# Chunked scan of a two-layer network: carried part of y scaled on its way out of PSUM, decays of all chunks worked out ahead, state scaled by ScalarE

## The reference

```python
dA = jnp.minimum(jnp.exp(dt * A[None, None, :]), 0.99)
def step(h, inp):
    x_t, B_t, C_t, dA_t = inp
    dBx = jnp.einsum('bhp,bn->bhpn', x_t, B_t)
    h = jnp.clip(dA_t[:, :, None, None] * h + dBx, -10.0, 10.0)
    y_t = jnp.einsum('bn,bhpn->bhp', C_t, h)
    return (h, y_t)
```

## Time and profile before

| | us |
|---|---|
| median of 3 runs | 1801.12 |
| the profiled execution, its own time | 1799.88 |
| its span in the profile | 1797.9 |
| TensorE busy | 1697.8 (94% of the span) |
| VectorE busy | 1588.3 (88%) |
| ScalarE busy | 1475.2 (82%) |
| the scan's chunks, from the first sums to the last maxima | about 1562 to 1704 |

### The profile page before, as it was taken

One profiled execution on the slowest core, in us unless ns is written; L12 is line 12 of the kernel. 1 busy time (PEld: TensorE's weight loads), 2 busy tenths in 40 slices (PEclk: granted clock), 3 DMA queues, 4 the chain that ended last, 5 costly groups with the idle time before them and its releaser, 6 DMA issues.

```text
span 1797.9 us, 40083 instructions
## 1 busy us (share of the span) xinstructions
PE 1697.8 (94%) x15396; PEld 660.0 (37%) x15396; DVE 1588.3 (88%) x2294; ACT 1475.2 (82%) x2806; POOL 642.7 (36%) x932
## 2 busy tenths in 40 slices
PE   6899999999999999999999999999999889899894
PEld 4432222222222222278722222222222345466663
DVE  7999999999999999945499999999998477588679
ACT  6689999999999999943389999999999757777555
POOL 2432300222444444100035566555610133123347
PEclk9999999999999999999999999999999989899887
DMA  4522221111211222278512211122102243422121
GB/s 127 176 72 88 86 74 59 57 59 39 72 57 55 59 69 61 69 209 227 153 47 57 64 48 48 50 64 56 41 12 57 68 125 112 138 69 71 40 76 47
DMA packets 152765, 142.15 MB, mean 79 GB/s; under 512 B 40394, under 2 KB 131533, under 8 KB 152418
## 3 DMA queue, kind: packets, MB, share of 16 engines
q1 hardware_dynamic: 144226, 122.37, 23.7%
q0 software_dynamic: 8352, 17.29, 3.3%
HBM read 76.60 MB, written 60.03 MB: 76 GB/s over the span
## 4 chain that ended last, share of the span: by engine, by line
PE 80%; ACT 9%; DVE 7%; issue 2%; POOL 1%; DMA 1%; SPq 0%; DVEq 0%; ACTq 0%
PE PS L2051 29%; PE PS L2150 18%; PE PS L2035 11%; ACT probs L1361 6%; PE PS L2100 4%; DVE mxp L910 3%; PE PS L2085 2%; PE PS L2355 2%; PE PS L2337 2%; PE PS L2273 1%; PE PS L2194 1%; PE PS L2200 1%; PE PS L2358 1%; PE PS L2077 1%; PE PS L2434 1%
## 5 line engine op out<-in xcount | busy, mean ns | idle before, releaser
L910 DVE TENSOR_REDUCE mxp<-PS 128x1 f32<-128x1024 f32 x1024 | 1170.5, 1215 | 19.0 <-PE PS L2035 14.6
L1361 ACT ACTIVATE probs<-PS 128x512 f32<-128x512 f32 x2048 | 1096.0, 597 | 65.4 <-PE PS L2150 21.4
L2051 PE MATMUL PS<-probs,VH 128*32 128x256 f32 x8192 | 642.0, 391 | 2.3 <-ACT probs L1361 1.0
L2150 PE MATMUL PS<-stacks 51*128 51x512 bf16 x2048 | 441.4, 388 | 20.3 <-ACT probs L1361 15.7
L2035 PE MATMUL PS<-stacks 48*128 48x512 bf16 x2048 | 416.5, 380 | 2.7 <-DVE mxp L910 1.7
L2051 PEld LDWEIGHTS PS<-probs,VH 128*32 128x32 f32 x8192 | 172.7, 108 | 404.5 <-issue 224.2
L2150 PEld LDWEIGHTS PS<-stacks 51*128 51x128 bf16 x2048 | 115.9, 93 | 459.9 <-ACT probs L1361 385.4
L1727 POOL DMA_INDIRECT S<-oe_d,ROWI x128 | 129.8, 1014 | 133.8 <-PE PS L2051 127.6
L1697 POOL DMA_INDIRECT xe_d<-S,ROWI x128 | 125.2, 978 | 137.8 <-PE PS L2051 119.5
L1675 POOL CAST spl<-nmx 128x8 bf16<-128x8 f32 x64 | 12.6, 197 | 303.5 <-DVE nmx L866 225.3
L2035 PEld LDWEIGHTS PS<-stacks 48*128 48x128 bf16 x2048 | 105.4, 95 | 16.9 <-DVE mxp L910 7.4
(11 more groups left out here) (363 smaller groups left out, 1813.7 us busy)
## 6 DMA issues: line engine op xcount, KB each, us to landing
stacks<-qkl_d SPq DMA_DIRECT2D x128, 96.0 KB
xe_d<-zt SPq DMA_DIRECT2D x16, 640.0 KB
XNT<-xe_d SPq DMA_DIRECT2D x32, 320.0 KB, 3.8
oe_d<-XNT SPq DMA_DIRECT2D x32, 320.0 KB, 3.3
stacks<-qkl_d SPq DMA_DIRECT2D x128, 64.0 KB
o_d<-SG SPq DMA_DIRECT2D x256, 32.0 KB
ews<-in_ew_dram SPq DMA_DIRECT2D x33, 192.0 KB, 2.4
stacks<-qkl_d SPq DMA_DIRECT2D x128, 32.0 KB
```

What stands on the lines that cost most here:

```text
L910: v.tensor_reduce(mxp[:, n // 2, n % 2:n % 2 + 1], MXB[n % 2].rearrange("p a c -> p (a c)"), X_AX, ALU.max).then_inc(mx_done, 1)
L1361: act.activation(probs[:, at:at + 512], PS[:, bank_of(u, e), :], ACT.Exp, scale=float(1.0 / np.sqrt(np.float32(DK)))).then_inc(exp_done, 1)
L2051: mm = pe.matmul(OB[32 * jg:32 * jg + 32, c:c + 256], VH[w][:, kt, :], probs[:, at:at + 256], start=(kt < 2 and half == 0), stop=(kt >= TC ...
L2150: pe.matmul(PS[:, bank_of(u, e), :], KS[w][o:o + KROWS + 3, kt * P:(kt + 1) * P], QS[w][o:o + KROWS + 3, q0:q0 + 512], start=True, stop=Tr ...
```

## The change

- The decays of all 16 chunks are summed once, ahead of the loop (`all_sums_`, eight matmul instructions in bank 5), and ScalarE takes their exponentials once (`all_exps`, four operations): `EC` (per token, for y), `ET` (per chunk, for the state), `ER` (rows for the bound). `ER` is stored to DRAM and read back as rows in four pieces (`load_rows`, two DMAs each, in SyncE's queue between the chunks' loads).
- The per-chunk L2340, L1551, L1552, L1553, L1096, L1120 and L1123 go, and L2358 with its 8 products.
- The carried part of y is now C times the unscaled state: one product per sequence, 256 columns wide, into bank 2 and bank 7 (`CY`). ScalarE copies it to `YS` in eight operations (2 sequences, 4 heads, 128x64 each) with the decay of the token as a per-partition scale. VectorE adds the part inside the chunk to it from banks 3 and 4. The old copy L1564 goes.
- The state is scaled by ScalarE in four operations of 128x64.
- TensorE waits, ahead of the second L2330, until ScalarE has read `CY` (`cy_out`), since both use bank 2. ScalarE's order is: exponentials and squares of c + 1, carried part of c, state of c, turned `DM` of c + 1, bound of c.

The diff, cut to its core:

```diff
             def spread_decays(c):
                 after(v, la_ready, c)
-                link(v.tensor_copy(ldc[:, :, :].unsqueeze(2), ldt[:, :, c:c + 1, :]))
-                v.tensor_tensor(lb, TRI..., ldc..., ALU.mult).then_inc(lb_set, 1)
+                v.tensor_tensor(lb..., TRI..., ldt[:, :, c, :].unsqueeze(3).broadcast_to([P, B, NH1, P]), ALU.mult).then_inc(lb_set, 1)
...
-                v.wait_ge(el_done, c + 1)
-                v.tensor_tensor(CTD[w], E2[w], cc, ALU.mult).then_inc(ops_ready, 1)
             def chunk_state(c):
-                v.tensor_tensor(hst2[:, :, :], HS[:, :, :], E2[c % 2][:, :, P - 1:P]..., ALU.mult).then_inc(hst_set, 1)
                 v.wait_ge(hst_set, HALVES + c + 1)
-                v.wait_ge(y_out, c + 1)
+                v.wait_ge(yc_ready, c + 1)
                 v.tensor_tensor(HS[:, :, :], hst2[:, :, :], PS[:, 3, DI:2 * DI]..., ALU.add).then_inc(hs_done, 1)
+                v.wait_ge(cy_out, c + 1)
+                yc = YS.rearrange("p (b c) n -> p b c n", b=B)[:, :, c:c + 1, :]
+                v.tensor_tensor(yc, yc, PS[:, 3:5, 0:DI].unsqueeze(2), ALU.add).then_inc(y_out, 1)
...
+            def all_exps():
+                act.wait_ge(all_sums, ALL_BASE + 1)
+                act.activation(EC, PS[:, 5, 0:NT * NH1], ACT.Exp)
+                act.activation(ET, PS[:, 5, 2 * P:2 * P + TCH * NH1], ACT.Exp)
+                act.activation(ER[:, 1:P], PS[:, 5, P:2 * P - 1], ACT.Exp)
+                act.activation(ER[:, 0:1], PS[:, 5, 2 * P - 1:2 * P], ACT.Exp).then_inc(rows_out, 1)
...
+            def state_scaled(c):
+                after(act, hs_done, c)
+                for h in range(NH1):
+                    ins = act.activation(hst2[:, h, :], HS[:, h, :], ACT.Copy, scale=ET[:, c * NH1 + h:c * NH1 + h + 1])
+                ins.then_inc(hst_set, 1)
+            def carried(c):
+                act.wait_ge(cy_ready, c + 1)
+                for b in range(B):
+                    for h in range(NH1):
+                        col = (b * TCH + c) * NH1 + h
+                        ins = act.activation(YS[:, b * TCH + c, h * HP:(h + 1) * HP], CY[b][:, h * HP:(h + 1) * HP], ACT.Copy, scale=EC[:, col:col + 1])
+                ins.then_inc(cy_out, 1)
...
             chunk_exps(0)
+            all_exps()
             router_exp()
+            chunk_turned(0)
             for c in range(TCH):
                 if c + 1 < TCH:
                     chunk_exps(c + 1)
+                carried(c)
+                state_scaled(c)
+                if c + 1 < TCH:
+                    chunk_turned(c + 1)
                 chunk_out(c)
...
             def chunk_products(c):
                 pe.wait_ge(ops_ready, c + 1)
                 if c + 1 < TCH:
                     turned(c + 1, 0)
+                carried(c)
                 after(pe, y_out, c)
-                after(pe, hs_done, c)
...
-                for h in range(NH1):
-                    for b in range(B):
-                        mm = pe.matmul(PS[:, 3 + b, h * HP:(h + 1) * HP], CTD[w][rows_of(b), h, :], HS[rows_of(b), h, :], start=False, stop=(h == NH1 - 1))
                 mm.then_inc(yc_ready, 1)
+                if c == ROUTER_CHUNK or c + 1 < TCH:
+                    pe.wait_ge(cy_out, c + 1)
                 if c == ROUTER_CHUNK:
                     router_rows()
                 if c + 1 < TCH:
                     turned(c + 1, 1)
...
+            hold(rows_out, ROWS_OUT + 1)
+            sp.dma_start(er_d.rearrange("b (n t) -> (b n) t", t=P), ER).then_inc(rows_st, 16)
             for w in range(2):
                 hold(zx_st[w], 32 * NT // 2)
             hold(bct_st, 32 * NB)
-            for c in range(2, TCH):
+            hold(rows_st, ROWS_ST + 16)
+            load_rows(0)
+            load_chunk(2)
+            load_chunk(3)
+            load_rows(1)
+            for c in range(4, TCH):
+                if c in (7, 11):
+                    load_rows(c // 4 + 1)
                 load_chunk(c)
```

More of the change, by code:

```diff
@@ L254, in build @@
         by_head = lambda t: t.rearrange("p (h t) -> p h t", h=NH1)
-        E2 = [by_head(probs[:, 0:512]), by_head(ym_flat[:, 2560:3072])]
-        CTD = [by_head(probs[:, 512:1024]), by_head(ym_flat[:, 3072:3584])]
-        E2b = [by_head(wa[2 + i].rearrange("p t c -> p (t c)")[:, 0:256].bitcast(BF16)) for i in range(2)]
+        EC, ET, ER = probs[:, 0:NT * NH1], probs[:, 128:128 + TCH * NH1], probs[:, 192:256].bitcast(BF16)
+        ERB = [waq[:, 2 * i:2 * i + 2, :, :].rearrange("p i t c -> p (i t c)").bitcast(BF16) for i in range(2)]
+        E2b = [t.rearrange("p (c h t) -> p c h t", c=TCH // 4, h=NH1) for t in ERB]
         XS = [probs[:, 1024:1536], probs[:, 1536:2048], SG[0][:, :], SG[1][:, :]]
@@ L263, in build @@
         BD = [heads(t) for t in (probs[:, 3072:3584], ym_flat[:, 2048:2560])]
-        ldc = sb("ldc", [P, B, NH1])
+        CY = [PS[:, 2, 2 * P:2 * P + DI], PS[:, 7, 0:DI]]
         HS = sb("HS", [P, NH1, HP])
@@ L380, in build @@
         SH_BASE = 2 * NB
-        yl_ready, pr_ready, s2_done = (
-            sem(n) for n in ("yl_ready", "pr_ready", "s2_done"))
+        yl_ready, pr_ready, cy_out = (
+            sem(n) for n in ("yl_ready", "pr_ready", "cy_out"))
         a1_ready, a1_out, l1_ready, oh_ready = (
@@ L654, in load_chunk, with load_rows @@
                 sp.dma_start(XS[w].rearrange("p (b n) -> p b n", b=B), bview(xs_d)).then_inc(tile_ld[w], 16)
+            def load_rows(k):
+                hold(c_done, 4 * (k - 1) if k >= 2 else 0)
+                for b in range(B):
+                    sp.dma_start(ERB[k % 2][b * DS:b * DS + 1, :], er_d[b:b + 1, k * 4 * NH1 * P:(k + 1) * 4 * NH1 * P]).then_inc(er_ld[k % 2], 16)
             def store_b_c(j):
@@ L1557, in chunk_exps, with chunk_turned @@
                     act.activation(RB[w][:, b, :, HP:P], BS[c % 4][:, b, :].unsqueeze(1).broadcast_to([P, NH1, DS]), ACT.Square)
+            def chunk_turned(c):
+                w = c % 2
                 act.wait_ge(dm_done, c + 1)
@@ L2336, in chunk_sums, with all_sums_, carried @@
                 for b in range(B):
-                    pe.matmul(PS[:, b, :], BELOW, scaled[:, b, :], start=True, stop=True)
-                after(pe, el_done, c)
-                for b in range(B):
-                    mm = pe.matmul(PS[rows_of(b), 7, :], onesq[:, 0:DS], scaled[:, b, :], start=True, stop=True)
-                mm.then_inc(la_ready, 1)
+                    mm = pe.matmul(PS[:, b, :], BELOW, scaled[:, b, :], start=True, stop=True)
+                mm.then_inc(la_ready, 1)
+            def all_sums_():
+                pe.wait_ge(zx_out, 2 * NT)
+                decays = DT.rearrange("p t h -> p (t h)")
+                pe.matmul(PS[:, 5, 0:P], TRI, decays, start=True, stop=True)
+                pe.matmul(PS[:, 5, P:2 * P], decays, TRI, start=True, stop=True)
+                for b in range(B):
+                    mm = pe.matmul(PS[rows_of(b), 5, 2 * P:2 * P + TCH * NH1], onesq[:, 0:DS], decays[:, b * TCH * NH1:(b + 1) * TCH * NH1], start=True, stop=True)
+                mm.then_inc(all_sums, 1)
+            def carried(c):
+                after(pe, cy_out, c)
+                after(pe, hs_done, c)
+                for b in range(B):
+                    mm = pe.matmul(CY[b], BCT[c % 4][rows_of(b), P:2 * P], HS[rows_of(b), :, :].rearrange("p h n -> p (h n)"), start=True, stop=True)
+                mm.then_inc(cy_ready, 1)
             def chunk_products(c):
@@ L2366, in chunk_products @@
                 for b, h, n in pairs:
-                    pe.matmul(PS[:, 5 + b, h * P:(h + 1) * P], DMb[w][:, b * NH1 + h, :], RB[w][:, b, h, :], start=(h == 0), stop=False)
+                    mm = pe.matmul(PS[:, 5 + b, h * P:(h + 1) * P], DMb[w][:, b * NH1 + h, :], RB[w][:, b, h, :], start=(h == 0), stop=(c == 0 and h == NH1 - 1))
                 after(pe, vr_out, 2 * c)
-                for b, h, n in pairs:
+                if c:
+                    pe.wait_ge(er_ld[c // 4 % 2], ER_BASE + 32 * (c // 8 + 1))
+                for b, h, n in pairs if c else ():
                     r = slice(b * DS, b * DS + 1)
-                    mm = pe.matmul(PS[:, 5 + b, h * P:(h + 1) * P], E2b[w][r, h, :], VR[r, h, :], start=False, stop=(h == NH1 - 1))
+                    mm = pe.matmul(PS[:, 5 + b, h * P:(h + 1) * P], E2b[c // 4 % 2][r, c % 4, h, :], VR[r, h, :], start=False, stop=(h == NH1 - 1))
                 mm.then_inc(c_done, 1)
```

37 lines of the change are left out of this document (18 added, 19 removed).

## The result

The changed kernel takes 1787.78 us (median of 4 runs, 1784.49 to 1789.78) against 1800.42 for the kernel before in the same comparison: ratio 0.9925, 95% interval 0.9911 to 0.9940. Forecast were 1786.4 us, and -14.7; measured -12.6. The profiled execution ran 1787.86, its span is 1785.9.

A forecast was written before the change was run, and what follows sets the result against it. TensorE bound the scan at 8.09 us per chunk; afterwards a TensorE-ScalarE round trip of 7.2 us would. Start -0.7, trips -10.7 and end -3.3 gave -14.7: median 1786.4 us, 8-in-10 range 1779 to 1796.

The forecast's parts named there:

- The trip: Mid-scan loop from ScalarE's exponential through the carried copies, TensorE's wait and next sums, back to ScalarE: 7.2 us per chunk.
- The price taken as half of two pointers: ScalarE's short operations, 64 columns with one scale pointer: 0.225 us from start to start, bounds 0.18 and 0.32.
- The engines' own sums: Busy time per chunk after the change: TensorE 6.54 us (7.0 at the other bound), VectorE 6.5, ScalarE 6.9.
- TensorE last at 6.6: Rival: cheaper ScalarE operations leave TensorE's own sum, 6.54 to 6.8 us, as the trip; 1777 to 1781 us, chance 0.14.
- no overlap on ScalarE: Rival: ScalarE's pointer operations take 0.32 us each, its trip 8.0; 1797 to 1800 us, close to no change, chance 0.08.
- The clock: Rival: short waits per chunk drop TensorE to half clock, +3.7 us a chunk, at worst 1855 us, chance 0.06.
- 14 trips: Scan, chunk 1 to 15: 100.8 us, plus 0.4 for the router and 2.0 for chunk 2's data; 103.2 against 113.9.
- My evidence against it: Against the clock's fall: a stretch with TensorE busy 6.24 of 8.00 us had clock 1.00; here 6.5 of 7.2.
- Chunk 2's wait: Chunk 2's loads land 1.1 to 1.9 us later, behind `ER`'s store and rows; TensorE loses 1.5 to 2.7, taken +2.0.
- The start: Chunk 1: L2340 goes (-1.0 us), the eight products of all decays cost +0.3; -0.7 in all.
- The last chunk: From chunk 15's exponential to the last maxima: 12.4 us, 14.6 with half clock, taken 13.5; -3.3.
- The rest: The stage after the scan: unchanged, only beginning earlier.

The follow-up runs named there:

- e_state_dve: The changed kernel with the state scaled by VectorE again instead of ScalarE: 1789.16 us, ratio 0.9927 to the kernel before.
- e_filler: The changed kernel with products whose result isn't read filling TensorE's wait for `cy_out`: 1781.56 us, ratio 0.9900 to the kernel before.
- e_half_signal: The changed kernel with `cy_out` given after each sequence's four copies, TensorE waiting only for the first: 1778.37 us, ratio 0.9884 to the kernel before.
- e_two_copies: The changed kernel with two unscaled copies of 256 columns instead of eight scaled ones, leaving the token's decay out: 1781.54 us, ratio 0.9893 to the kernel before.
- c_before: The kernel before, unedited, profiled a second time: start 6.06 us, 14 trips 115.56, last 17.34, rest 93.5.
- v_early: e_half_signal with chunk 2's x and B loads ahead of the wait for the last stores, all six ahead of the decay rows: 1772.53 us, ratio 0.9840 to the kernel before.
- c_after: The changed kernel, unedited, profiled a second time: 1787.9 us, ratio 0.9935 to the kernel before.
- e_before_fill: The kernel before with four unread products filling TensorE's wait ahead of chunk 1's sums: 1799.32 against 1799.05 us, ratio 0.9994.
- v_pool: The changed kernel with the half signal, chunk 2's loads ahead of the decay rows, and the state scaled by GpSimd: 1777.58 us, ratio 0.9865 to the kernel before.
- e_pad: The changed kernel with 16 tiny memsets on VectorE ahead of the first chunk: 1788.04 us, ratio 0.9942 to the kernel before.

## Why the prediction was right

**The trip** is the forecast: 7.17 against 7.2, and for the reason given; e_state_dve, e_filler and e_half_signal bear it out from three sides. ScalarE's exponential and squares took the 2.06 of the forecast (1621.99 to 1624.05). Two terms were off and nearly cancelled: the eight copies take 1.74 to the last one's end, not 1.90 (0.196 apart, not 0.225), and the L2330 behind the wait 0.48, not 0.28 to 0.42. The price taken as half of two pointers, 0.225, was 0.015 low for the copies from SBUF (0.24) and 0.03 high for those from PSUM. The Trainium skill (ScalarE: Activation LUTs, "What ACT_TABLE_LOAD costs") makes no difference between the two sources; an estimate from its figures is 0.239 for both, which fits the state and is 0.04 too high for the copies from PSUM. The engines' own sums were right too: VectorE 6.51 (forecast 6.5), ScalarE 6.8 (6.9), TensorE 6.61 in e_two_copies (6.54).

**The rivals.** TensorE last at 6.6 and no overlap on ScalarE: neither came. The clock came in part, and it is the term that the sum lacked: I took 14 trips as 100.8 + 0.4 + 2.0 = 103.2; the profiles have 111.5 and 107.7. With the short waits filled (e_filler) and no fall in the trips they took 103.35. A fall cost 4.4 behind chunk 2's wait in one profile, 1.7 to 2.7 in the router's chunk and 1.7 in one or two others. So the trips gave 5.1, not 10.7. The Trainium skill (TensorE: Matmul & The Clock Gate, "A second HAM failure mode: psum-queue depth-cycling") tells of another kernel in which short idles between groups of products make the clock swing; the falls in mid-scan and their absence with the filler agree, the two falls without an idle (c_before, v_early) aren't of that kind. My evidence against it, one stretch with gaps at full clock, showed only that falls aren't certain, and the trace of the kernel before already had, besides the fall in its last chunk, one behind the wait ahead of chunk 1's sums. In its timeline:

```profile
1568.26 3.58 PE L2337 MATMUL PS<-VP,cst 128*128 128x512 f32 x4 [1.15 <-DVE VP L1097]
```

**Chunk 2's wait** was 2.0 in the sum and cost 1.93 in c_after, but by luck. Counted from chunk 0's exponential the data were forecast for 15.2 to 15.9 us and wanted at 12.6; TensorE went on at 13.9 and 13.5, and had wanted them at 10.9. The six loads weren't late because of the new store and rows: they began at 7.8 and 7.5, in the two profiles of before at 7.4 and 10.4. The scan reached them sooner.

**The start** gave 1.8, not 0.7: the products of all decays stand exactly where TensorE waited, and L2379 of chunk 1 took 1.97 where it had taken 3.58. e_before_fill shows that filling this place holds the clock. The forecast counted them as a cost of 0.3.

**The last chunk** gave 1.7, not 3.3: 15.5 and 15.2, worse than the 14.6 that I had for half clock, though TensorE stood only 0.98 us for the state, not 1.8. With the filler it took 12.8, near the 12.4 forecast for full clock.

**The rest**, which the forecast took as unchanged, gave 4.3 by the profiles. 0.6 of it lies ahead of the flag, where the first operation on the maxima takes 0.38 instead of 0.97; in e_filler and v_pool it takes 1.0 again. From the flag to VectorE's first addition of the output stage (L1253; L1271 after) it is 18.3 and 17.4 us in the two profiles of before, 13.8 and 14.3 in the two of the changed kernel, and from there to the end of the span 74.1 in all four. Of these 3.8 us 2.3 are VectorE's gap behind the flag. The other 1.5 are on TensorE, which has to wait for VectorE's first gate operations. In the timeline of the kernel before:

```profile
1711.73 1.11 PE L2411 MATMUL PS<-ident,VH 128*128 128x128 f32 x4 [0.92 <-DVE wff L1198]
...
1714.31 3.62 PE L2434 MATMUL PS<-HH,ews 128*128 128x512 f32 x4
```

The same in the changed kernel's:

```profile
1703.07 1.52 PE L2467 MATMUL PS<-ident,VH 128*128 128x128 f32 x8
1704.43 1.88 PE L2490 MATMUL PS<-HH,ews 128*128 128x512 f32 x4
```

There the wait is gone, the clock is back one product sooner, and four products take 1.88 instead of 3.62. The gap moves with what VectorE's program holds ahead of it (e_pad); what follows on TensorE, not always: e_state_dve, whose gap is 4.06, has the waits and the 3.62 and takes 18.3 as before, e_pad has the waits (0.91 and 1.02) but 1.88, and takes 15.7. So 1.7 us of the 3.8 are shown to go with the gap, and why the clock was still down in the one and not in the other stays open. So does how much of it is in the median: neither of the two is slower than c_after by more than can be told.

So the total, 12.6 against 14.7, is nearer than its terms, and that is luck: 5.6 too much in the trips and 1.6 in the last chunk are made up by 1.1 at the start and 4.3 in a stage that the sum left out (by the profiles, whose sum is 13.0).

## What to carry to other kernels

When an engine is relieved, write down the closed loop through every new wait, with all that is queued behind the waiting instruction; it, not the largest sum, set the new time here, and signalling as soon as the half that matters was done gave 9.5 us more. A wait of half a microsecond per trip cost a nearly full TensorE more than itself, since it made falls of the clock more frequent; even useless products in it paid. When a loop gets faster, look at what is loaded for its first trips: cover that was enough at 8.1 us per chunk wasn't at 7.2, and issuing that chunk's largest load first, ahead of the wait for stores that it didn't need, removed the wait.

## What was unexpected of the hardware

- The clock also fell on a TensorE with no gap at all: L2337 3.66 us at 1600.83 in c_before, with the engine busy from 1592 to 1610, and L2383 3.68 us at 1602.64 in v_early.
- After the branch on the flag VectorE took 1.73 or 1.74 us to its next operation in nine profiles and 4.04 to 4.27 in five; 16 memsets added to its program took it from 1.74 to 4.17. Why an operation 130 us earlier does that, no run here shows.
- One GpSimd operation of 128x256 beside VectorE slowed a VectorE operation from 1.21 to 1.63 us and took 1.60 itself, against 0.61 or 0.62 in the three trips of v_pool in which the two didn't overlap.
